# Routing waits by bank, token slots found inside an attention, a causal layer begun pair by pair

## The reference

```python
def _L1_ffn_ref(hidden, gate_w, Wg, Wu, Wd, Ws_g, Ws_u, Ws_d):   # 16 experts choose tokens
    scores = softmax(einsum('bsd,ed->bse', hidden, gate_w)).transpose(0, 2, 1)
    topk_w, topk_idx = top_k(scores, 14)          # 14 = 112 * 2 / 16 tokens of each sequence
    x_tok = hidden gathered at topk_idx
    eo = ((gelu(x_tok @ Wg) * (x_tok @ Wu)) @ Wd) * topk_w
    return eo scattered and added at topk_idx + shared expert(hidden)

def _L2_ffn_ref(x, ...):                          # two causal layers
    for l in range(2):
        x = x + attn(ln(x, ln1[l]))               # causal, 16 heads of 16
        h = ln(x, ln2[l])
        moe = _token_moe if l % 2 == 0 else _seq_moe   # top 2 of 8 experts, by token or by sequence
        x = x + moe(h)
```

## Time and profile before

| | |
|---|---|
| median of 3 executions | 1651.27 us (1649.63 to 1653.52) |
| profiled execution, whole | 1646.45 us |
| its span, first to last instruction | 1645.1 us |
| TensorE busy | 1543.9 us, 94% of the span |
| VectorE, ScalarE, GpSimd busy | 749.0, 680.6, 243.1 us |
| mean granted clock of TensorE | 0.97 of full |

### The profile page before, as it was taken

One profiled execution on the slowest core, in us unless ns is written; L12 is line 12 of the kernel. 1 busy time (PEld: TensorE's weight loads), 2 busy tenths in 40 slices (PEclk: granted clock), 3 DMA queues, 4 the chain that ended last, 5 costly groups with the idle time before them and its releaser, 6 DMA issues.

```text
span 1645.1 us, 32380 instructions
## 1 busy us (share of the span) xinstructions
PE 1543.9 (94%) x12111; PEld 1275.4 (78%) x12111; DVE 749.0 (46%) x2647; ACT 680.6 (41%) x2152; POOL 243.1 (15%) x382
## 2 busy tenths in 40 slices
PE   7999999799999999998899978999999999999986
PEld 5787887688987777776699967779987787777765
DVE  3536465510126676766111167760134443444466
ACT  2615433221107767565233335733334443344452
POOL 2022201000001121213311142164000000000000
PEclk9999999899899999999799999989999999999999
DMA  9300011348600211420799810337820001000000
GB/s 309 126 1 1 1 43 38 116 165 285 137 1 18 58 56 56 166 92 16 253 331 332 290 43 17 104 112 260 298 86 1 1 2 38 1 1 1 1 1 23
DMA packets 103378, 159.79 MB, mean 97 GB/s; under 512 B 12244, under 2 KB 80972, under 8 KB 102612
## 3 DMA queue, kind: packets, MB, share of 16 engines
q1 hardware_dynamic: 97544, 146.68, 27.0%
q0 software_dynamic: 3648, 9.44, 1.7%
q10 hardware_dynamic: 2048, 1.84, 0.3%
HBM read 150.72 MB, written 14.81 MB: 101 GB/s over the span
## 4 chain that ended last, share of the span: by engine, by line
PE 74%; ACT 8%; DVE 4%; issue 3%; DMA 2%; POOL 1%; POOLq 0%; ACTq 0%; DVEq 0%
PE psum L588 46%; PE psum L685 6%; PE psum L669 5%; PE psum L709 5%; PE psum L975 5%; ACT arena L896 4%; DMA expert_out<-arena 1%; PE psum L962 1%; PE psum L544 1%; POOL token_rows L1287 1%; ACT arena L910 1%; PE psum L717 1%; PE psum L554 1%; DVE arena L808 1%; PE psum L1709 0%
## 5 line engine op out<-in xcount | busy, mean ns | idle before, releaser
L896 ACT ACTIVATE arena<-arena,rowmin 112x375 f32<-112x375 f32 (+1 forms) x584 | 292.6, 508 | 182.1 <-DVE rowmin L808 182.0
L588 PE MATMUL psum<-arena,region 128*128 128x112 f32 (+2 forms) x1920 | 324.7, 326 | 3.4 <-DVE x_state L2232 1.7
L588 PEld LDWEIGHTS psum<-arena,region 128*128 128x128 f32 x1920 | 261.4, 196 | 63.9 <-DVE x_state L2232 3.0
L588 PE MATMUL psum<-region,arena 128*125 128x128 f32 (+4 forms) x1632 | 231.6, 292 | 9.6 <-DVE arena L797 3.3
L588 PEld LDWEIGHTS psum<-region,arena 128*125 128x125 f32 (+2 forms) x1632 | 196.1, 184 | 44.2 <-issue 18.7
L685 PEld LDWEIGHTS psum<-identity,arena 112*125 112x125 f32 (+1 forms) x1240 | 142.0, 177 | 58.4 <-ACT arena L910 17.2
L685 PE MATMUL psum<-identity,arena 112*125 112x112 f32 (+1 forms) x1240 | 166.0, 278 | 15.9 <-ACT arena L910 5.0
L588 PE MATMUL psum<-arena 128*128 128x128 f32 (+4 forms) x896 | 141.4, 315 | 0.0
L669 PE MATMUL psum<-arena 32*112 32x375 f32 (+3 forms) x912 | 133.8, 479 | 0.5 <-DVE arena L786 0.4
L588 PEld LDWEIGHTS psum<-arena 128*128 128x128 f32 (+2 forms) x896 | 125.8, 192 | 10.6 <-issue 0.3
L956 POOL COPY arena<-rinv 112x128 f32<-112x128 f32 x136 | 33.9, 293 | 582.1 <-DVE rinv L831 559.3
(11 more groups left out here) (320 smaller groups left out, 1903.0 us busy)
## 6 DMA issues: line engine op xcount, KB each, us to landing
stream<-in_moe_w SPq DMA_DIRECT2D x36, 1024.0 KB, 7.3
arena<-in_moe_w SPq DMA_DIRECT2D x36, 1024.0 KB, 7.4
arena<-in_ctxT SPq DMA_DIRECT2D x32, 375.0 KB, 4.4
stream<-in_e_wg SPq DMA_DIRECT2D x8, 512.0 KB, 4.5
stream<-in_e_wu SPq DMA_DIRECT2D x8, 512.0 KB, 5.7
stream<-in_e_wd SPq DMA_DIRECT2D x8, 512.0 KB, 6.6
region<-in_e_wg SPq DMA_DIRECT2D x8, 512.0 KB, 7.7
region<-in_e_wu SPq DMA_DIRECT2D x8, 512.0 KB, 8.6
```

What stands on the lines that cost most here:

```text
L588: last = pe.matmul(dst, l, r, start=(i == 0), stop=(i == n - 1))
L896: last = act.activation(e, e, ACT.Exp, bias=rowmin[:, j, n:n + 1], scale=-1.0, accum_out=rowsum[:, j, h:h + 1])
```

## The change

It has three parts. (A) The conversion of the first eight indices moves ahead of the second search; the spreading products wait for eight indices, then for the rest, and signal each bank; each compare waits for its bank; the experts' loop begins when two of eight `selT` copies are made, its second slot when five are. (B) The count of turn 0's picks (one column instead of 112) goes in front of the scores of step 5 of the second attention, the three slot products in front of those of step 6, both into free columns of bank 0; VectorE copies, multiplies there, and reduces and casts in its last step; ScalarE's copy goes. GpSimd writes lanes 0 and 1 of turn 0 before the roots of the second norm, lanes 2 and 3 behind them, and turn 1 when its slots are there. (C) The second causal layer takes statistics of three lanes, applies lanes 0 and 1, then does lane 3; TensorE runs 22 fillers, transposes lanes 0 and 1, makes their keys and queries, and then does the same for lanes 2 and 3. Helpers get the arguments `lanes_of`, `beside` and `midway`; signals of the numbered steps shift.

```diff
@@ -530,9 +534,9 @@
-        def norm_apply(v, p, it, r, src, dst):
-
-            for j in range(LANES):
+        def norm_apply(v, p, it, r, src, dst, lanes_of=range(LANES)):
+
+            for j in lanes_of:
                 if j % 2 == 0:
...
@@ -543,10 +547,10 @@
-        def turn(pe, p, it, r, rn, src, idle=0, free=None):
+        def turn(pe, p, it, r, rn, src, idle=0, free=None, lanes_of=range(LANES)):
...
             keep_busy(pe, bank_t[3], idle)
-            for j in range(LANES):
+            for j in lanes_of:
                 if free is not None and free(j) is not None:
...
@@ -666,6 +671,8 @@
                         rhs = kT[j][rows, 0:a.keys]
+                    if j == 0 and beside is not None and r in beside:
+                        beside[r]()
                     pe.matmul(bank_s[j][0:T, 0:a.group * a.keys], lhs, rhs, start=True, stop=True)\
...
@@ -718,6 +725,8 @@
             for j in range(LANES):
+                if j == 2 and midway is not None:
+                    midway()
                 keys_queries(0, j)
...
@@ -1273,19 +1284,25 @@
             p = p_f[0]
-            for it in range(ITERS):
-                attend_gpsimd(g, af[0], p, it)
-                norm_rstd(g, p, 0, it)
-
-            g.wait_ge(s_zero, 16)
-            for i in range(ITERS):
-                g.wait_ge(s_route, 5 if i == 0 else 9)
-                g.wait_ge(*p["normed"].at(0, f_norms(0)[NORM_A2 + i], LANES - 1))
-                for j in range(LANES):
+            def scatter(i, lanes_of):
+                for j in lanes_of:
                     for k in range(TOP2):
...
                                              hrow[j][:, i, :], None).then_inc(s_scat, 16)
+
+            attend_gpsimd(g, af[0], p, 0)
+            norm_rstd(g, p, 0, 0)
+            attend_gpsimd(g, af[0], p, 1)
+            g.wait_ge(s_zero, 16)
+            g.wait_ge(s_route, 5)
+            g.wait_ge(*p["normed"].at(0, f_norms(0)[NORM_A2], LANES - 1))
+            scatter(0, (0, 1))
+            norm_rstd(g, p, 0, 1)
+            scatter(0, (2, 3))
+            g.wait_ge(s_route, 9)
+            g.wait_ge(*p["normed"].at(0, f_norms(0)[NORM_B2], LANES - 1))
+            scatter(1, range(LANES))
             g.wait_ge(s_tid, 4)
...
@@ -1493,9 +1510,6 @@
                     attend_scalar(act, af[l], p, it, own=(1,) if it else ((1, 2, 4, 5), (4, 5, 6))[l])
-                    if l == 0 and it:
-                        act.wait_ge(s_rmm, 1)
-                        act.copy(count[0:P // 2, :], bank[4][0:P // 2, 0:T]).then_inc(s_route, 1)
                     if l == 0:
...
@@ -1696,11 +1710,13 @@
-            pe.wait_ge(s_topstep, 7)
             for c in range(CAP):
+                if c % 8 == 0:
+                    pe.wait_ge(s_topstep, 7 if c else 4)
                 last = pe.matmul(bank[4 + c // 4][0:T, c % 4 * P:(c % 4 + 1) * P],
                                  topf[:, c:c + 1].broadcast_to([P, T]), ident[:, :], start=True, stop=True)
-            last.then_inc(s_rpe, 1)
+                if c % 4 == 3 or c == CAP - 1:
+                    last.then_inc(s_rpe, 1)
...
@@ -1725,11 +1741,13 @@
-            pe.wait_ge(s_selTk, B)
+            pe.wait_ge(s_selTk, 2)
             with pe.Fori(0, E1 // EX_SLOTS) as i:
...
                         pe.wait_ge(s_ew[n], i * 48 + 48)
+                        if n:
+                            pe.wait_ge(s_selTk, 5 if n == 1 else B)
                         if n >= 2:
...
@@ -1834,34 +1852,45 @@
-            def slots_of(i, to):
+            def slots_of(i, to, held):
...
                 held_by = slice(0, (i + 1) * P // 2)
-                pe.matmul(to[0:T, 0:P // 2], before, picked[:, of], start=True, stop=False)
-                pe.matmul(to[0:T, 0:P // 2], count[held_by, :], groups_before[held_by, of], start=False, stop=False)
-                pe.matmul(to[0:T, 0:P // 2], whole_of.broadcast_to([E2, T]), chunks_before[:, of], start=False,
+                pe.matmul(to, before, picked[:, of], start=True, stop=False)
+                pe.matmul(to, held, groups_before[held_by, of], start=False, stop=False)
+                pe.matmul(to, whole_of.broadcast_to([E2, T]), chunks_before[:, of], start=False,
                           stop=True).then_inc(s_rmm, 1)
+
+            def count_of_first():
+                pe.wait_ge(s_picks, TOP2)
+                pe.matmul(bank_s[0][0:P // 2, 256:257], picked[:, 0:P // 2], one_col[0:T, 0:1], start=True, stop=True)\
+                    .then_inc(s_rmm, 1)
+
+            def slots_of_first():
+                pe.wait_ge(s_rconst, 16 * 7)
+                pe.wait_ge(s_route, 2)
+                slots_of(0, bank_s[0][0:T, 256:256 + P // 2], count_first.broadcast_to([P // 2, T]))
+                pe.wait_ge(s_rmm, 2)
...
                 for it in range(ITERS):
-                    turn(pe, p, it, 0, (at_norm[NORM_A + it]) - it * p["normed"].times, first[it], 0 if it else ([0, 32][l]),
-                         (lambda j: p["xT_ready"].at(0, 1, 3 if j == 2 else j) if l == 1 and j < 3
-                          else p["g_val"].at(0, 0, j)) if it else None)
+                    tokens = l == 1 and it == 0
+
+                    def turn_first(idle, lanes_of):
+                        turn(pe, p, it, 0, (at_norm[NORM_A + it]) - it * p["normed"].times, first[it], idle,
+                             (lambda j: p["xT_ready"].at(0, 1, 3 if j == 2 else j) if l == 1 and j < 3
+                              else p["g_val"].at(0, 0, j)) if it else None, lanes_of)
+
+                    turn_first(22 if tokens else 0, range(2) if tokens else range(LANES))
                     attend_tensor(pe, af[l], p, it, 0, lambda j: xT[j], None,
                                   lambda j: add_on(pe, j, row2(l, "bo"), more=accs[j][:, it, :]),
-                                  None if it or l else lambda j: p_l2x["x_added"].at(ITERS - 1, 0, j))
+                                  None if it or l else lambda j: p_l2x["x_added"].at(ITERS - 1, 0, j),
+                                  beside={5: count_of_first, 6: slots_of_first} if l == 0 and it else None,
+                                  midway=(lambda: turn_first(0, range(2, LANES))) if tokens else None)
                     project_out(pe, p, it, 0, w_f[l][3], lambda j: p["o_T"].at(it, af[l].tiles - 1), onto=True)
-                    if l == 0 and it:
-                        pe.wait_ge(s_picks, TOP2)
-                        pe.matmul(bank[4][0:P // 2, 0:T], picked[:, 0:P // 2], one_col[0:T, 0:1].broadcast_to([T, T]),
-                                  start=True, stop=True).then_inc(s_rmm, 1)
-                        pe.wait_ge(s_rconst, 16 * 7)
-                        pe.wait_ge(s_route, 2)
-                        slots_of(0, bank[5])
                     if l == 1:
...
@@ -2199,23 +2228,23 @@
             v.max_index(topi16[:, 0:8], top16[:, 0:8], scoreT).then_inc(s_topstep, 1)
-            v.wait_ge(s_topstep, 2)
+            v.wait_ge(s_topstep, 3)
+            v.tensor_copy(topf[:, 0:8], topi16[:, 0:8]).then_inc(s_topstep, 1)
             v.max(top16[:, 8:16], scoreT2).then_inc(s_topstep, 1)
-            v.wait_ge(s_topstep, 4)
+            v.wait_ge(s_topstep, 5)
             v.max_index(topi16[:, 8:16], top16[:, 8:16], scoreT2).then_inc(s_topstep, 1)
-            v.tensor_copy(topf[:, 0:8], topi16[:, 0:8]).then_inc(s_topstep, 1)
             v.wait_ge(s_topstep, 6)
             v.tensor_copy(topf[:, 8:CAP], topi16[:, 8:CAP]).then_inc(s_topstep, 1)
-            v.wait_ge(s_rpe, 2)
             for k in range(4):
                 n = min(4, CAP - 4 * k)
+                v.wait_ge(s_rpe, 2 + k)
                 v.tensor_scalar(sel[:, 4 * k:4 * k + n, :], three(bank[4 + k][0:T, 0:n * P], n), iota[0:T, 0:1],
...
             for b in range(B):
-                v.wait_ge(s_rpe, 2 + B + b + 1)
+                v.wait_ge(s_rpe, 5 + B + b + 1)
                 v.tensor_copy(selT[:, b, :, :], three(bank[b][0:T, 0:2 * T], 2)).then_inc(s_selTk, 1)
...
@@ -2326,12 +2355,20 @@
-            def norm_of_tokens(p, it, add=False):
+            def stats_of_tokens(p, j):
+                add_tokens(0, j)
+                v.wait_ge(s_tokadd, TOP2 * (j + 1))
+                v.bn_stats(stats[:, j, :], accs[j][:, 0, :]).then_inc(p["stats_done"].sem, 1)
+
+            def aggregate_tokens(p, lanes_of):
+                for j in lanes_of:
+                    v.wait_ge(*p["stats_done"].at(0, 0, j))
+                    v.bn_aggr(mv[:, j, :], stats[:, j, :]).then_inc(p["var_ready"].sem, 1)
+
+            def norm_of_tokens(p, it):
...
                     for j in range(2 * h, 2 * h + 2):
-                        if add:
-                            add_tokens(it, j)
                         v.wait_ge(s_tokadd, it * SEQ_ITEMS + TOP2 * (j + 1))
...
@@ -2359,11 +2396,26 @@
+            def keep_count_of_first():
+                v.wait_ge(s_rmm, 1)
+                v.tensor_copy(count_first, bank_s[0][0:P // 2, 256:257]).then_inc(s_route, 1)
+
```

(30 more changed lines are left out.)

## The result

The changed kernel took 1635.97 us in the median of four runs (1632.91 to 1638.77), against 1652.39 for the kernel before in the same set (1649.63 to 1655.46): a ratio of 0.9892, 95% interval 0.9868 to 0.9915. It is faster by 16.4 us in the medians, where I had forecast 7.7 with a range whose lower end was 1639.5. The direction was right, the size was too small by half, and the time lies outside the range.

The account below looks back on a forecast made before the run. TensorE, with 74% of the chain, was taken as the bound, so edits pay only where the chain leaves its large products. Gains 5.5 + 1.3 + 0.9 = 7.7 us off 1651.27 gave 1643.6, range 1639.5 to 1648.5.

Parts of the forecast that it names:

- The reasoning on the clock: Block 2's gather: with the idle gap cut to 0.5 us the clock should stay up, gaining another 1.9 us.
- some executions of today's kernel may not lose it: Block 2's gather: the clock's fall is tied to nothing in the program, so the 1.9 us loss may be absent.
- at most 0.7: Block 2: sign that gather records start at most 0.7 us after the last index record.
- Rival 3: Block 2 compares do not overlap, second causal layer's lead is lost to ScalarE; total gain 2.6 us, 1648.7; chance 0.10.
- rival 1: Second causal layer's opening: clock falls, 1.5 us on the path and 0.9 gain not had; 1646.0 us; chance 0.15.
- last slot cast, behind the attention's first mask: Passage to the scatter: work taken out starts the cast 1.6 us earlier, work put in costs 0.4.
- last write behind that cast: Scatter: the second eight indirect writes start about 1.0 us after their cast; 1.5 us earlier overall, 1.3 taken.
- they start about 1.0 after their cast (as the first did): Scatter: delay from slot cast to the second eight writes, read from the first write, 772.51 to 773.48.
- From the last write on, its landing (5.43) and the fetch of rows after it are unchanged.: Behind the scatter: no gain or loss expected in the 5.43 us landing or the fetch of rows.
- rival 2: First chunks: rows share transfer engines with weights, hiding the early slots' gain; total gain 4.6 us, 1646.7; chance 0.12.
- The warning of the Trainium skill: Moved indirect writes in the attention: VectorE can lock GpSimd out and stretch them; the prediction changed no term for it.
- Rival 4: Step 6 of the second attention: constant tables land late; 1656.6 us at 30 us of delay; chance 0.03.

Follow-up runs that it names:

- e9: Changed kernel with the bank-by-bank routing of block 2 taken back; 1633.55 us, ratio 0.9962 to the kernel before.
- e4: Kernel before with only the early slots of the second attention, all sixteen indirect writes together behind the reciprocal roots; 1639.26 us, ratio 0.9986.
- e1: Kernel before with only the bank-by-bank routing of block 2 added; 1637.66 us against 1641.35, ratio 0.9975.
- e3: Kernel before with only the pair-by-pair opening of the second causal layer added; 1641.46 us, ratio 0.9993.
- e8: The kernel before run again without an edit; 1654.36 us, ratio 1.0002.
- e10: Changed kernel with the early slots and split writes of the second attention taken back; 1635.78 us, ratio 0.9965 to the kernel before.
- e2: Kernel before with only the early slots and split writes of the second attention added; 1637.85 us against 1641.35, ratio 0.9984.
- e5: The changed kernel run again without an edit; 1634.51 us against 1654.56 for the kernel before, ratio 0.9896.
- e6: Changed kernel with the pair-by-pair opening of the second causal layer taken back; 1640.82 us, ratio 0.9932 to the kernel before.
- e11: Changed kernel with eight filler products ahead of a down projection in the tail; 1629.12 us, ratio 0.9926 to the kernel before.
- e12: The changed kernel once more without an edit, on another chip; 1630.73 us against 1642.19 for the kernel before, ratio 0.9939.
- e16: Changed kernel with 40 filler products ahead of the first transposes of the first causal layer; 1637.48 us, ratio 0.9981 to the kernel before.
- e14: Kernel before with SyncE's weights for chunk slots 2 and 3 waiting for the first rows to land; 1639.35 us against 1642.45, ratio 0.9989.
- e7: Changed kernel without the ten filler products ahead of the first chunk's rows; 1644.36 us, ratio 0.9931 to the kernel before.
- e13: Changed kernel with SyncE's weights for chunk slots 2 and 3 waiting for the first rows to land; 1631.71 us, ratio 0.9944 to the kernel before.

## Why the prediction was wrong in size

In short: the steps of A and C held, and B was priced at a quarter of what it brought. Its terms ahead of the scatter's landing were too small, and the passage behind the landing, which I had called unchanged, was not. The measured 16.4 us are more than all three parts account for, and what is left over is not shown.

**Part A: right.** Forecast 5.5, bounds 4.1 and 6.0. Eleven profiles with A show 14.27 to 14.92 us, mean 14.6; seven without it fall in two groups, 17.90 to 18.20 (three) and 20.23 to 21.73 (four), mean 19.9. So A is worth 5.3 on average. The two groups are the clock over the gather: in e9 it was 0.50 over most of the gather, and the 32 records, 6.32 us in e4, took some 9.5. The idle ahead of the gather was 2.55 us in all seven, whether the clock fell behind it or not. The reasoning on the clock held, and "some executions of today's kernel may not lose it" was right, in three of seven. The gap ahead of the gather was 0.80 and not "at most 0.7"; the clock was 1.00 in every gather of A. Rival 3 is out.

**Part C: right.** Forecast 0.9; nine of eleven profiles gained 0.85 on average (10.65 against 11.50), two gained nothing when the clock fell. I had given this rival 1 a chance of 0.15, which fits, but priced it at 1.5 us on top of the 0.9 not had, and no such loss is seen (11.47 and 11.44 against 11.50). Mean 0.7.

**Part B: wrong, 1.3 forecast, about 5 found.** This is the difference of the means of the five profiles without it (before, e1, e3, e8, e10) and of the eight with it whole (e2, e5, e6, e9, e11, e12, e16, after): 5.6 from the last mask on, 5.3 without the 0.33 that this mark flatters. Without e8, whose stage "rows" is spoiled by the stall, it is 4.6. Term by term:

| step | forecast | measured |
|---|---|---|
| last slot cast, behind the attention's first mask | 1.2 earlier | 1.9 (52.9 to 51.1) |
| last write behind that cast | 0.3 earlier | 1.2 (10.2 to 9.0) |
| landing | 0 | 0.4 later (6.3 to 6.7) |
| request for rows to the first chunk's products | 0 | 1.6 earlier (8.3 to 6.75); without e8 0.5 (7.2) |
| the first chunk's products | 0 | 1.1 shorter (12.5 to 11.5); without e8 1.4 (12.9) |

- The first two were mis-sized. The 1.2 was 1.6 for the work taken out less 0.4 for the work put in. Of the 0.4 almost nothing reached the chain: the last mask is 0.33 later in every profile with B, but the projection behind the attention starts 37.03 us after the first mask where it started 36.98. The fillers behind the projection start 1.85 us earlier, not 1.6. And "they start about 1.0 after their cast (as the first did)" was the wrong row to take: the first write of a group that GpSimd comes to first was 0.97 us behind its cast again (753.91 + 0.26 to 755.14), the second group's 0.27. Together this is 3.0 before the landing instead of the 1.3 taken. e4 shows that 1.7 of it is the split alone.
- The step that failed outright is the sentence "From the last write on, its landing (5.43) and the fetch of rows after it are unchanged." SyncE's weights for slots 2 and 3 wait for the scatter and for ScalarE's last accumulator copy of the first layer; GpSimd's request for the rows waits for the scatter alone. In before the scatter landed last, both requests went at once, and the weights won by 0.1 us. With B the copy comes last in six of eight profiles, by 1.1 to 2.2 us, and the rows are on their way before those weights are asked for. I had seen in rival 2 that rows and weights share the engines, but took it as a reason for a smaller gain. How much of this is B's doing is not shown, though: the copy also came last in four of the six profiles without B (e1, e8, e10 and e14). In e2 and e11, where the weights still went first, "rows" is 7.01 and 7.90.
- The last row of the table is the clock under the first chunk: 11.12 us where it was up, 12.2 to 13.7 where it was not. It was up in six of the eight profiles with B and in two of five without (e8, e10). These are the eight in which the copy came 0.9 us or more behind the scatter: the fillers start 0.82 us behind the later of the two, and a late start lets them reach to the landing of the rows, so that TensorE has no idle stretch ahead of the transposes. e7 shows the fillers' part, 1.5 us. e10 has all of it with no B, so B makes it more likely and does not ensure it.

The timed runs agree with the size only loosely. The parts alone (e1, e2, e3) come to 7.9 us by their ratios, which is the forecast's 7.7; each part taken out of the whole (e6, e9, e10) costs 6.0, 3.8 and 4.3 us by the ratios, 14.1 together. Every one of these six has an uncertainty of 3 us or more.

The warning of the Trainium skill that I weighed ("SBUF — State Buffer", two separate sides) does not show in this trace: the moved writes stand 1.26 and 1.24 us apart beside VectorE's work (756.65, 757.91, 759.15), as the writes of the scatter behind 773.48 did.

**The sum.** 5.3 + 5.3 + 0.7 = 11.3, or 10.6 without e8's passage, and e12, with neither the stall nor the short tail in its profile, says 11.5 in its medians and 10.0 by its ratio. The first set says 16.4 (interval 14 to 22), and e5 17.2 by its ratio. The stall was in the profiles of both, and can't be the gain itself, as it is in either kernel. What these two share beside it is a tail of 571.0 to 571.1 in the changed kernel's profile where e8 and before have 574.5 to 574.7: 3.5 us that no edit of this change made, in four of sixteen profiles without e11's fillers, e14 among them, which is almost the kernel before. And e8, a profile of the kernel before in such a set, loses 1.4 in A and 2.3 from the cast to the first chunk's output against the first one of before. 11.3 + 3.5 + up to 3.7 covers the 16.4; that the timed runs are made up as these few profiles are was not shown.

The median that I subtracted from, 1651.27, lies with the slower set by its size, while the profile that I read, 1646.45, has no stall. I carried the 4.8 us between them along as a constant. That two executions of one kernel can differ by a stall of 8 us and by 3.5 us in the tail was a thing to ask of a second profile.

**Rival 2** (B hidden anyway) is out: with B alone (e2) the first chunk's output came 4.4 us earlier. **Rival 4** (constants late) is out: the slots' products ran at 743.99 to 744.58 with nothing waiting for the constants.

## What to carry over

Where one queue waits for one event and another for that event and a second one, an edit that changes which of the two comes last also changes who is served first; list, for each request behind the moved step, what else is released with it. Price a step that is freed by the nearest row of the same position in its queue, not of the same kind. Choose marks that the edit itself does not move: here the last mask moved by 0.33 us. And before two profiles, or a profile and a median, are set against each other, compare them stage by stage: here one stage was 8.7 us longer in one of them for reasons that lie outside the kernel.

## What the runs showed of the hardware that I had not expected

- TensorE's instructions came one every 0.3 to 1.4 us for some 6 us, always at the same fillers, in either kernel, in the profile of after and every profile of one set of runs, and in none of three other sets, one of them on the same chip; with the half clock after it this cost 8 to 10 us. In the same five profiles SyncE's instructions came one every 0.7 us for some microseconds ahead of the first chunks, and in e8 ScalarE stood idle for 10.80 us. No transfer or semaphore that I found in the trace accounts for it, and its cause is open.
- The same idle 2.94 us in the tail was followed by a granted clock of 0.50 in twelve profiles and of 1.00 in four. Neither the edit nor the time at which it is reached sorts them. Filling it moved the fall to another place, and 2 of the 3.5 us of the loss were won (e12's 574.54 to 572.52).
- Rows asked for ahead of the weights for two chunks were transposed 4.2 to 5.4 us after their request, in twelve profiles; asked for 0.1 us behind them, 5.6 to 6.6, in five. Forcing the order by a wait on the other queue cost nothing that the time shows, and won nothing that it shows either (e13, e14).
- Behind the same idle 2.55 us ahead of the gather, the granted clock fell in four of seven profiles and stayed at 1.00 in three (9.5 or 7.9 us for the 32 records against 6.32).
